# State sum of a selective scan by accumulating fp32 transposes, in a fused scan and mixture-of-experts kernel

## What is computed

```python
u     = silu(conv4(in_proj(ctx)))                 # [b, e, l]
dt_lo, Bm, Cm = x_proj(u)                         # 8, 16 and 16 rows
delta = softplus(dt_proj(dt_lo) + dt_proj_b)      # [b, e, l]
# over l, for each state n:
state = state * exp(delta * A) + (delta * u) * B
y     = sum over the 16 states of state * C       # [b, e, l]
y     = (y + D * u) * silu(layernorm(x))
x     = x + transpose(y)                          # [b, l, e]
# then a mixture of 8 experts, 2 per row, capacity 320 rows each:
probs = softmax(layernorm(x) @ Wg); gates, experts = top_k(probs, 2)
out   = x + sum_k gate_k * (relu(rows @ w1[e_k]) @ w2[e_k])
```

## Time and profile before

| | |
|---|---|
| runs | 354.39, 355.7, 356.2 us; median 355.7 us |
| the profiled execution | its span is 353.9 us, from the first to the last instruction; its own device time isn't given apart |
| busy | PE 276.9 us (78%), PEld 242.0 (68%), DVE 266.8 (75%), POOL 234.3 (66%), ACT 170.6 (48%) |
| mean granted TensorE clock | 0.891 of full speed |
| preparation / scans / end of the scans to the first expert's rows / experts | to about 42 us / 42 to 190 us / 190 to 231 us / 231 to 354 us |

### The profile page before, as it was taken

One profiled execution on the slowest core, in us unless ns is written; L12 is line 12 of the kernel. 1 busy time (PEld: TensorE's weight loads), 2 busy tenths in 40 slices (PEclk: granted clock), 3 DMA queues, 4 the chain that ended last, 5 costly groups with the idle time before them and its releaser, 6 DMA issues.

```text
span 353.9 us, 5109 instructions
## 1 busy us (share of the span) xinstructions
PE 276.9 (78%) x1684; PEld 242.0 (68%) x1684; DVE 266.8 (75%) x373; ACT 170.6 (48%) x308; POOL 234.3 (66%) x144
## 2 busy tenths in 40 slices
PE   7889187746456588666669698889999999999970
PEld 6334175635346377555569688889999999999970
DVE  1489999999999999999997664167566675857610
ACT  0498366654825423327741236084647474554600
POOL 0125999987799948443548248738686777768643
PEclk9969679896959986988888879999999999999995
DMA  7940000000030000000005502654645545454210
GB/s 253 303 115 3 0 0 1 2 0 0 0 119 3 0 0 2 0 1 2 1 15 210 189 23 100 217 179 172 245 161 190 184 148 183 159 216 174 89 49 33
DMA packets 13504, 33.10 MB, mean 94 GB/s; under 512 B 2602, under 2 KB 9268, under 8 KB 11216
## 3 DMA queue, kind: packets, MB, share of 16 engines
q1 hardware_dynamic: 10240, 25.92, 21.7%
q0 software_dynamic: 2816, 6.32, 5.1%
q10 hardware_dynamic: 432, 0.65, 0.7%
HBM read 25.50 MB, written 8.43 MB: 96 GB/s over the span
## 4 chain that ended last, share of the span: by engine, by line
PE 33%; DVE 31%; issue 15%; DMA 8%; POOL 5%; ACT 4%; SPq 1%; POOLq 0%; DVEq 0%
DVE h L1061 16%; PE ps L864 9%; PE ps L866 8%; PE ps L865 8%; DVE hc L1072 4%; POOL expert_rows L316 4%; DMA xnat<-in_x 2%; PE ps L680 2%; DMA w1raw<-in_w 2%; PE ps L873 2%; DMA expert_rows<-xrow,sloti 2%; PE ps L882 1%; DVE dbu L1180 1%; DVE delta L1026 1%; PE ps L851 1%
## 5 line engine op out<-in xcount | busy, mean ns | idle before, releaser
L293 POOL TENSOR_TENSOR dbu<-du,bsb 128x1024 f32<-128x1024 f32 x30 | 101.1, 3392 | 29.0 <-DVE h L1061 23.1
L1061 DVE TENSOR_TENSOR_SCAN h<-da,dbu 128x1024 f32<-128x1024 f32 x32 | 100.6, 3144 | 0.1
L680 PEld LDWEIGHTS ps<-cst,hc 128*128 128x128 f32 x512 | 74.7, 225 | 5.5 <-issue 2.2
L680 PE MATMUL ps<-cst,hc 128*128 128x128 f32 x512 | 74.6, 309 | 0.0
L673 PE MATMUL ps<-stack,sels 96*128 96x512 bf16 x32 | 14.4, 451 | 55.3 <-DVE hc L1072 55.3
L1252 DVE SCALAR_TENSOR_TENSOR htlo<-ps,hthi 128x320 fp32r<-128x320 f32 x64 | 30.4, 486 | 34.1 <-ACT hthi L588 34.0
L462 ACT ACTIVATE bsb<-ps 128x512 f32<-128x512 f32 x32 | 18.8, 593 | 63.1 <-PE ps L667 61.9
L348 POOL TENSOR_TENSOR w2lo<-w2raw,w2hi 128x512 fp32r<-128x512 f32 x30 | 38.2, 1300 | 12.8 <-ACT w2hi L579 12.6
L673 PEld LDWEIGHTS ps<-stack,sels 96*128 96x128 bf16 x32 | 3.2, 101 | 63.0 <-DVE hc L1072 54.1
L480 ACT ACTIVATE da<-delta,anegs 128x510 f32<-128x510 f32 x64 | 41.9, 712 | 0.0
L864 PE MATMUL ps<-xthi,w1hi 128*128 (+1 forms) x128 | 40.6, 317 | 1.0 <-DVE w1lo L1169 1.0
(11 more groups left out here) (142 smaller groups left out, 483.2 us busy)
## 6 DMA issues: line engine op xcount, KB each, us to landing
w1raw<-in_w SPq DMA_DIRECT2D x8, 1024.0 KB
w2raw<-in_w SPq DMA_DIRECT2D x8, 1024.0 KB, 4.8
expert_rows<-fill SPq DMA_DIRECT2D x1, 2580.0 KB, 17.8
xe<-expert_rows SPq DMA_DIRECT2D x8, 258.0 KB, 5.7
xnat<-in_x SPq DMA_DIRECT2D x1, 1024.0 KB, 8.7
out<-x SPq DMA_DIRECT2D x2, 512.0 KB, 4.1
sels<-in_sel SPq DMA_DIRECT2D x1, 768.0 KB, 9.9
xe<-expert_rows SPq DMA_DIRECT2D x8, 64.5 KB, 5.5
```

Source lines behind the costliest of these rows:

```text
L293: nc.gpsimd.tensor_tensor(dbu[r][:], du[:, :, halves(hb)], bsb[r][:, None, :].to_broadcast([P, EC, HT]), ALU.mult).then_inc(s["dbu_done"], 1)
L680: ins = nc.tensor.matmul(y[:, t, c * P:(c + 1) * P], hc[par][:, c, t * P:(t + 1) * P], ident, start=False, stop=last, skip_group_check=True)
L1061: nc.vector.tensor_tensor_scan(h[r][:].rearrange("p c t -> p (c t)"), da[r][:].rearrange("p c t -> p (c t)"), dbu[r][:].rearrange("p c t - ...
```

## The change

The matmuls of `add_state` become transposes: the same operands, the same places in PSUM, the same order and semaphores, and still accumulated (start=False). No instruction moves on any engine.

```diff
@@ add_state @@
                 for t in tiles:
                     for c in range(EC):
                         ins = nc.tensor.matmul(y[:, t, c * P:(c + 1) * P], hc[par][:, c, t * P:(t + 1) * P],
-                                               ident, start=False, stop=last, skip_group_check=True)
+                                               ident, start=False, stop=last, is_transpose=True,
+                                               skip_group_check=True)
                 return ins
```

## The result

| | before | changed |
|---|---|---|
| median of 20 runs | 355.75 us | 356.87 us |
| lowest to highest | 354.39 to 356.87 | 355.47 to 358.9 |
| ratio | | 1.0031, 95% interval 1.0016 to 1.0046 |
| span of the profiled execution | 353.9 us | 354.9 us |
| mean granted clock | 0.891 | 0.777 |

The kernel became 1.1 us slower. So the forecast of no change was wrong, and the question is where a microsecond came from when 20 us of PE's busy time in one group were saved.

A forecast was written before the change was run, and what follows sets the result against it. DVE was taken to bound the scans, busy 147.34 of 148.00 us. Terms of 0 in the scans, 0 at their end and 0 in the experts left the span at 353.9 us and the median at 355.7 us, range 354.5 to 357.1.

The forecast's parts named there:

- The cost of one sum: State sum on PE: a transpose is one record instead of two, making a sum 0.91 us shorter at full clock, 1.71 at half.
- D: Rival on the state sums: an accumulating transpose costs two records, so the time stays 355.7 us; chance 0.04.
- The scans, 0: Steps 1 to 28: nothing waits for the sums, so 29 to 55 us saved become idle time at the C row, worth 0.
- the 25 announced: Sign of being right: PE's wait at the C row in the scans grows from 55.3 us by 25 us or more.
- DVE 1.25 us earlier at the end: End of the scans: shorter last sums let the gate start at about 192.1 us instead of 193.35.
- So the 1.25 us end in a longer wait before L851, and are worth 0: Expert 0's rows: L851 waits for a transfer until 201.06 us, so DVE's earlier end gains 0.
- The side effect, taken as 0: DVE's two additions, moved to 193.5 us, might hold up an earlier send by 0 to 0.64 us; 0 was taken.
- Rival A: PE's clock falls with less work; low from 184 us on, it makes L851 0.7 us late, 356.4 us; chance 0.16.
- The rule on transposes and the clock: Skill's rule that full clock does not engage for transposes; by it the scans would be at half clock throughout.
- The chances: Whole kernel: 0.88 within 0.5% of no change, 0.06 faster, 0.06 slower; the forecast itself 0.68.

The follow-up runs named there:

- e1: The changed kernel with the state sums of steps 28 to 31 made products with the identity again; 354.64 us, ratio 0.9984.
- e3: The changed kernel with 16 more clock matmuls behind the last logits, in PE's idle time before expert 0's rows arrive; 354.3 us, ratio 0.9971.
- e6: The changed kernel (transposes) with the second half's counts moved ahead of L851 in PE's queue; 352.51 us, ratio 0.9912.
- e9: The kernel before (products) with 8 more clock matmuls behind the last logits; 353.5 us, ratio 0.9923.
- e11: The changed kernel (transposes) with 13 clock matmuls added behind the last logits; 354.12 us, ratio 0.9953.
- e12: The kernel before (products) with 8 more clock matmuls behind the last logits, run once more; 353.78 us, ratio 0.994.
- e10: The kernel before with every second block row left out of each state sum, four products a step; one execution, 357.06 us, only the scans comparable.
- e2: The kernel before with transposes in the state sums of steps 28 to 31 alone; 356.79 us, ratio 1.0049.

## Why the prediction was wrong

- **The cost of one sum: right.** One record for a transpose, 1.04 us for eight at full clock and 1.91 at half were worked out; 1.04 and 1.92 were measured. D is out.
- **The scans, 0: right.** DVE is as full as before, and steps are 4.29 us. (The experts don't hold most of PE's busy time: from 211 us on it is 129 of 276.9 us. Nothing hung on that.) The idle time at the C row grew only from 55.3 to 60.5 us, not by the 25 announced: at half clock PE uses up what it saves. e1 shows that this costs nothing.
- **DVE 1.25 us earlier at the end: right** in the profiled execution, 1.15. Sum 28 took 1.92 us and not the 1.4 worked out, but nothing waited for it. In e3 and e6, where the clock fell again at the end, it was 0.9 and 0.1 us, counted from the first send.
- **"So the 1.25 us end in a longer wait before L851, and are worth 0": this step failed.** The wait is indeed longer, 3.90 us. But I treated waiting as free. While PE waited the clock fell, at 200.3 us, and L852 behind the wait is on the path: 3.58 us instead of 3.07. I took the 3.07 us of L851 as a length that would stay, and did not ask at which clock it ran. It was a mixture, since the clock fell at 201.6 us in the midst of it; at full clock throughout, the same 12 records take 2.05 us (e9, e11, e12). My spacings of 0.112 and 0.213 us would not have priced it: 11 x 0.112 + 0.275 = 1.5 us and 11 x 0.213 + 0.42 = 2.8 us are both too little, as these records don't all start that close together.
- **The side effect, taken as 0: failed too.** It was sized 0 to 0.64 us and was 0.51. I chose the lower end because the eighth send was not delayed by the same additions. But it depends on where a send's start falls against them, and the additions had moved by over a microsecond. That eighth send was issued 0.13 us before the end of the first addition and waited for that one alone; the seventh of the changed kernel was issued when the second had just started. The row that was nearest was the third send with 3.02 us, which ended 0.8 us after the scan that was running when it was issued. The same 0.8 us hold for the additions.
- **Rival A** had about the right loss (0.7) by the wrong road. The clock did fall in the scans, and there it cost nothing. At the end it was back at 1.00 from 186.7 us on in the profiled execution, and the gate was early, not late. A price was put on PE being too slow at the end, and none on its being too early. A's fall of the clock at the end does occur, in the traces of e3 and e6, but there too the logits ended before the rows had come.
- **The rule on transposes and the clock** (the Trainium skill, "TensorE: Matmul & The Clock Gate", section "Part 4: PE-mode transpose"): the fall in the scans looks like it. e10 doesn't need the rule, since products in the same number led to the same clock, 0.58 and 0.57 over the scans. No run here has transposes alone in a number that keeps PE full, so the rule as a whole isn't tested.
- **The chances.** 0.88 on no change over 0.5% held by the number, 0.31%. Both failed terms had the same sign; one stood in the range alone, the other nowhere. That 356.87 us lies inside the range is luck in part: its upper end was made of rival A's 0.7 us, which didn't come, and the 0.51 us of L852 happened to fit into their place.

## What to carry to other kernels

When work moves off the path, price what the new idle time does: the first instructions behind a longer wait on PE may start at half clock. Ask too what the earlier instructions will now run beside. Then look for what stands in the queue behind the wait: here, moving the counts ahead of the wait for the transfer turned a loss of 1.1 us into a gain of about as much, by the medians.

## What the runs showed of the hardware

- Transposes of fp32 blocks accumulate in PSUM on a running fp32 sum, also mixed with products in one sum (e1, e2). Each is one record where a product is two, 0.11 against 0.22 us at full clock.
- Eight transposes or four products a step led to the same granted clock, 0.50 over 20 us of steady steps, whereas eight products a step had 0.87 in the same 20 us of the kernel before, and 1.00 in the last 14 of them.
- The granted clock stayed at 1.00 for a while after PE had fallen idle: in the changed kernel PE was idle from 197.4 us and the clock fell at 200.3. In the kernel before PE was idle from 199.1 to 201.06 and it fell at 201.6, when PE was at work again. It came back at 208.5 us there and at 210.6 in the changed kernel, though PE was busy without a break from 204 us on in both.
- An indirect DMA issued by POOL lasted 0.97 us alone. Issued during a DVE addition of two SBUF operands (512 elements), it ended 0.84 to 0.85 us after that addition, but never lasted less than 0.97, and so took 0.97 to 1.48 us; during a scan of 800 or 1,024 elements it lasted 1.47 and 2.15 to 3.02 us. During a multiply or gate with one operand in PSUM it lasted 0.97 to 0.98 us.
- Clock matmuls in 2 to 3 us of idle time bring 12 fp32 records from 3.07 or 3.58 us down to 2.05, and the whole kernel 2.1 to 2.8 us, as the records behind are at full clock too (e9 and e12 against the kernel before, e11 against the changed kernel).
